# Adapter by roles on one Trainium2 core: the order of the first loads, splits and turns ahead of the steady loop

## The reference

```python
h = einsum('bsh,bhk->bsk', x, W_down[role]) + b_down[role][:, None, :]   # H = 1024 -> K = 512
h = gelu(h, approximate=False)
u = einsum('bsk,bkh->bsh', h, W_up[role]) + b_up[role][:, None, :]       # K = 512 -> H = 1024
y = x + u
yn = (y - mean(y)) * rsqrt(var(y) + 1e-5)                                # over H
out = yn * gamma[role][:, None, :] + beta[role][:, None, :]
```

## Time and profile before

| | us |
|---|---|
| median of three runs | 1424.69 |
| lowest, highest | 1423.2, 1425.12 |
| the profiled execution's own time | 1424.26 |
| its span in the trace | 1422.4 |
| TensorE busy in the span | 1405.7 |
| VectorE busy | 1203.8 |
| ScalarE busy | 782.5 |
| GpSimd busy | 195.1 |

### The profile page before, as it was taken

The page is one execution under the profiler, slowest core; times in us unless marked ns, Lnnn a source line. Parts: engine busy times, 40 slices in busy tenths (PEclk is TensorE's granted clock), DMA queues, the critical chain, the costliest instruction groups (busy, mean ns, idle before and its releaser), DMA issues.

```text
span 1422.4 us, 32330 instructions
## 1 busy us (share of the span) xinstructions
PE 1405.7 (99%) x6175; PEld 1156.3 (81%) x6176; DVE 1203.8 (85%) x1454; ACT 782.5 (55%) x2059; POOL 195.1 (14%) x297
## 2 busy tenths in 40 slices
PE   8999999999999999999999999999999999999997
PEld 6888888888888888888888888888888888888885
DVE  7798988888888888888888899888888888888888
ACT  5555555555555555555555555555555555555555
POOL 3376411100000000000000377310100000000000
PEclk9999999999999999999999999999999999999999
DMA  9688777766666666666666778776776666667663
GB/s 222 177 232 229 217 211 205 199 199 205 185 190 197 196 182 196 196 197 183 188 204 192 209 230 225 222 201 193 204 217 186 197 203 185 184 194 203 187 193 139
DMA packets 208726, 283.52 MB, mean 199 GB/s; under 512 B 25775, under 2 KB 155312, under 8 KB 208702
## 3 DMA queue, kind: packets, MB, share of 16 engines
q1 hardware_dynamic: 201726, 269.60, 63.5%
q0 software_dynamic: 5888, 12.07, 5.1%
q10 hardware_dynamic: 1088, 1.57, 0.4%
HBM read 183.27 MB, written 99.88 MB: 199 GB/s over the span
## 4 chain that ended last, share of the span: by engine, by line
PE 96%; DVE 1%; DMA 1%; issue 1%; ACT 1%; SPq 0%; DVEq 0%
PE p_down L989 16%; PE p_down L990 16%; PE p_down L991 16%; PE p_up L989 16%; PE p_up L990 16%; PE p_up L991 16%; DMA row<-in_L_cond_W_down 0%; DVEq L241 0%; SPq L267 0%; SPq L258 0%; DMA h_quad<-h_dram 0%; DMA h_dram<-h 0%; DVE row L805 0%; PE p_hT L985 0%; DVE x_quad L921 0%
## 5 line engine op out<-in xcount | busy, mean ns | idle before, releaser
L989 PE MATMUL p_down<-wd_hi,xT_hi 128*128 x1012 | 395.4, 391 | 0.2
L991 PE MATMUL p_down<-wd_hi,xT_lo 128*128 x1012 | 393.9, 389 | 0.0
L990 PE MATMUL p_down<-wd_lo,xT_hi 128*128 x1012 | 393.9, 389 | 0.0
L989 PE MATMUL p_up<-wu_hi,hT_hi 128*128 x1008 | 392.7, 390 | 0.1
L991 PE MATMUL p_up<-wu_hi,hT_lo 128*128 x1008 | 392.3, 389 | 0.0
L990 PE MATMUL p_up<-wu_lo,hT_hi 128*128 x1008 | 392.3, 389 | 0.0
L559 ACT ACTIVATE hT_hi<-p_hT 128x512 fp32r<-128x512 f32 x126 | 75.5, 599 | 435.4 <-DVE p_hT L724 432.6
L744 DVE SCALAR_TENSOR_TENSOR row<-p_up,row 128x1024 f32<-128x1024 f32 x126 | 154.2, 1224 | 170.8 <-PE p_up L991 135.1
L989 PEld LDWEIGHTS p_down<-wd_hi,xT_hi 128*128 128x128 f32 x1012 | 189.9, 188 | 45.0 <-issue 5.2
L989 PEld LDWEIGHTS p_up<-wu_hi,hT_hi 128*128 128x128 f32 x1008 | 189.2, 188 | 42.0 <-issue 1.6
L991 PEld LDWEIGHTS p_down<-wd_hi,xT_lo 128*128 128x128 f32 x1012 | 190.0, 188 | 39.9
(11 more groups left out here) (164 smaller groups left out, 955.6 us busy)
## 6 DMA issues: line engine op xcount, KB each, us to landing
x_quad<-in_x SPq DMA_DIRECT2D x510, 128.0 KB, 3.6
row<-in_x SPq DMA_DIRECT2D x126, 512.0 KB, 4.1
out<-row SPq DMA_DIRECT2D x126, 512.0 KB, 2.8
h_dram<-h SPq DMA_DIRECT2D x125, 256.0 KB, 4.3
h_quad<-h_dram SPq DMA_DIRECT2D x500, 64.0 KB, 2.0
w_raw<-in_L_cond_W_down POOLq DMA_DIRECT2D x64, 64.0 KB, 3.7
w_raw<-in_L_cond_W_up POOLq DMA_DIRECT2D x64, 64.0 KB, 3.8
row<-in_L_cond_W_up SPq DMA_DIRECT2D x16, 128.0 KB, 5.8
```

Of the source, the lines that this page charges most:

```text
L989: pe.matmul(dst, a_hi, w_hi, start=first, stop=False)
L990: pe.matmul(dst, a_hi, w_lo, start=False, stop=False)
L991: return pe.matmul(dst, a_lo, w_hi, start=False, stop=last)
```

## The change

ScalarE's queue issues quads 0 and 1 of piece 2 of W_down directly behind piece 1, ahead of the wait for `first_known` and of its two quads of x of sequence 0. Lo of piece 1 is made in two subtractions of 128 x 512 (`split_chunk`), one ahead of `subtract_half(0, 0)` and one behind it, with a semaphore of its own for the first. `transpose_half(0, 1)` moves from behind `transpose_half(0, 0)` to behind `transpose_half(1, 0)`, and `round_half(0, 1)` and `subtract_half(0, 1)` move behind those of (1, 0). GpSimd clears half of `xT_lo`, and TensorE does two matmuls of 512 columns on these zeros ahead of its wait for `first_hi`. Of the four `keep_clock` matmuls behind the spreads two are left, and the second of them waits for `half_hi`, which is the rounding of (0, 0).

```diff
@@ gpsimd
             pool.memset(opener[:, 0:2], 0.0).then_inc(pieces_split, 1)
+            pool.memset(xT_lo[:, 0:HALF, :].bitcast(F32), 0.0).then_inc(zeros_ready, 1)
@@ scalar
             load_first(act, 0, range(1, NQ))
             load_first(act, 1)
+            load_first(act, FD - 2, range(0, NQ // 2))
             act.wait_ge(first_known, 1)
...
             round_first(0)
-            load_first(act, FD - 2, range(0, NQ // 2))
             act.wait_ge(order_in_psum, 1)
...
             round_first(1)
             round_half(0, 0)
-            round_half(0, 1)
             copy_param(2, p_up[1][:, :], BETA, H, beta_loaded)
             copy_param(1, p_hT[:, :], BD, K, bias_loaded)
             round_half(1, 0)
+            round_half(0, 1)
             round_first(2)
@@ vector
+            def split_chunk(n, c, done):
+                buf, hi, lo, _ = first_piece(n)
+                at = slice(c * K, c * K + K)
+                dve.wait_ge(first_hi, n + 1)
+                dve.tensor_tensor(lo[:, at], buf[:, at], hi[:, at].bitcast(F32), ALU.subtract).then_inc(done, 1)
...
             def subtract_half(b, half):
                 hi, lo = half_x(b, half)
+                if (b, half) == (0, 0):
+                    dve.wait_ge(zeros_used, 1)
...
             split_first(0)
             transpose_half(0, 0)
-            transpose_half(0, 1)
+            split_chunk(1, 0, chunk_split)
             subtract_half(0, 0)
-            split_first(1)
+            split_chunk(1, 1, first_split)
             dve.wait_ge(first_known, 2)
             for b in range(2):
                 params_at[b], when_loaded[b] = first_slot(b)
             transpose_half(1, 0)
+            transpose_half(0, 1)
+            subtract_half(1, 0)
             subtract_half(0, 1)
-            subtract_half(1, 0)
             transpose_half(1, 1)
@@ tensor
+            pe.wait_ge(zeros_ready, 1)
+            for _ in range(2):
+                mm = pe.matmul(p_down[:, :], xT_lo[:, 0, :], xT_lo[:, 0:HALF, :], start=True, stop=True)
+            mm.then_inc(zeros_used, 1)
             pe.wait_ge(first_hi, 1)
             keep_clock(2)
...
-            keep_clock(4)
+            keep_clock(1)
+            pe.wait_ge(half_hi, 1)
+            keep_clock(1)
             pe.wait_ge(first_known, 2)
...
                 for c in range(half * HALF, half * HALF + HALF):
-                    if b == 0 and c % (FC // K) == 0:
+                    if (b, c) == (0, FC // K):
+                        pe.wait_ge(chunk_split, 1)
+                    elif (b, c) == (0, FC // K + 1):
+                        pe.wait_ge(first_split, 2)
+                    elif b == 0 and c % (FC // K) == 0:
                         pe.wait_ge(first_split, c // (FC // K) + 1)
```

More of the change, by code:

```diff
@@ L143, in adapter_kernel @@
         param_rows_clear, row_known = sem("param_rows_clear"), sem("row_known")
+        zeros_ready, zeros_used, chunk_split = sem("zeros_ready"), sem("zeros_used"), sem("chunk_split")
         ident_ready, params_spread, params_landed = sem("ident_ready"), sem("params_spread"), sem("params_landed")
```

## The result

The changed kernel takes 1427.68 us (median of 11 runs, 1426.1 to 1430.27) against 1424.95 us (11 runs, 1423.11 to 1425.33): ratio 1.0024, 95% interval 1.0016 to 1.0032. It is slower by 2.7 us, outside the predicted range. The profiled execution took 1426.3 us itself, 2.0 more than the profiled one of before, and is among the quickest of the changed kernel's runs.

What follows compares the result with a forecast made beforehand. The prediction took TensorE (busy 99%) as the bound, with VectorE deciding turn_h(0). Its terms summed to +0.8 us on the profiled 1424.26, 1425.1, set at 1425.2 as the median lies 0.43 above that execution; range 1423.5 to 1426.8.

Steps and rivals of the forecast that it cites:

- TensorE's own program would allow 13.5: Ahead of the first product: keep_clock pair at 8.58, seven spreads and two fillers let TensorE start it at 13.5 us.
- Product (0,0) starts 0.2 behind the subtraction's end ... 13.8: First product on TensorE: starts 0.2 us after VectorE's subtraction ends at 13.6, so at 13.8 us.
- the lower clock: Rival, chance 0.06: a break of some 0.3 us at 13.5 keeps first-product matmuls slow, 2.3 us; sum 3.1, time 1427.4.
- x turned at 11.46: VectorE's turn of sequence 0's x: lands and is turned at 11.46 us instead of 10.40, behind piece 2.
- The dear bound: Delay of sequence 0's x by piece 2: 256 KB at 242 GB/s, 1.06 us; the forecast took this bound.
- the hole is filled: Rival, chance 0.22: piece 2 partly fills the DMA dip at 6 to 7 us, x only 0.57 late; 1424.5 us.
- Even turns: Rival, chance 0.16: DMA queues share evenly, x of sequence 0 lands at 12.5, +1.7 us, time 1426.0.
- The zeros by 3.8: Two TensorE matmuls on zeros: end by 3.8 us, ahead of the sort's first matmul, at no cost.
- Turn of (1,0) at 14.5 with "issue" as releaser: VectorE's turn of (1,0): held by L840's register loads, 1.6 us, until 14.5 instead of 14.06.
- VectorE's chain, 6.4 us to the turn of (2,0): VectorE from turn of (1,0) to turn of (2,0): 6.4 us, ending at 20.9 to 21.0 against 20.17, 0.8 late.
- turn_h(0) at 25.8: TensorE's turn_h(0): starts at 25.8 us instead of 24.99, 0.8 later, set by VectorE's chain.
- every microsecond by which turn_h(0) comes earlier or later stays in the time: From turn_h(0) on: TensorE's matmuls have no hole to hide a shift, so it goes wholly into the time.

Runs made afterwards that it cites:

- e1: Changed kernel with TensorE's three register loads and their wait for first_known moved ahead of the wait for half_hi: 1425.51 us, ratio 1.0007 to the kernel before.
- e6: Kernel before with only piece 2's two quads issued ahead of x on ScalarE's queue: 1423.8 against 1423.61 us, ratio 1.0002.
- e12: e1 with turn, rounding and subtraction of (0,1) in their old place: 1425.21 against 1424.62 us for the kernel before, ratio 1.0007.
- e2: Changed kernel with piece 2's two quads issued behind round_first(0) again, so x goes first: 1424.39 us, ratio 1.0005 to the kernel before.
- e10: Kernel before with only the later turn, rounding and subtraction of (0,1): 1424.66 against 1424.62 us, ratio 1.0000.
- e3: Changed kernel with nine keep_clock matmuls instead of one behind the wait for half_hi: 1425.59 us, ratio 1.0012 to the kernel before.
- e8: e5 with VectorE's register loads for sequences 2 and 3 behind the bias of sequence 0: 1424.36 against 1423.61 us for the kernel before, ratio 1.0002.
- e5: Changed kernel with the edits of e1 and e2 together: 1425.36 against 1423.61 us for the kernel before, ratio 1.001.
- e4: Kernel before with its four keep_clock matmuls replaced by one, the wait for half_hi, and one: 1425.72 us, ratio 1.0007.
- e7: Kernel before with only the zeros added (GpSimd's memset and two matmuls): 1424.1 against 1423.61 us, ratio 1.0001.
- e11: Kernel before with zeros, two fillers instead of four, and VectorE's register loads for sequences 2 and 3 behind sequence 0's bias: 1424.08 against 1424.62 us, ratio 0.9996.

## Why the prediction was wrong

The step that failed is "TensorE's own program would allow 13.5", on which "Product (0,0) starts 0.2 behind the subtraction's end ... 13.8" rests. The subtraction ended at 13.95, and the product started at 15.73. The prediction followed the matmuls of TensorE's program, seven spreads and two fillers, and not the instructions between them. It named what the change queues behind `pe.wait_ge(half_hi, 1)` only as one filler; three register loads stand there too, and with their arithmetic they take 2.3 us. So the break ahead of the product was 2.0 us, where the prediction had "some 0.3 us", and in the profiled execution it brought the lower clock, the rival to which the prediction had given a chance of 0.06. It had applied that very question to VectorE (the loads of L840, priced at 1.6 us) and not to TensorE. e1 moves these loads, and the product, the turns and turn_h(0) come within 0.2 us of the forecast: that step is shown, not argued.

The others, in order:

- *round_first(0) at 7.45*: 7.42, right.
- *x turned at 11.46*: 11.78 in the changed kernel, 11.52 in e1, 11.40 in e6. The dear bound held, so "the hole is filled" fell: the dip was filled (227 GB/s), and x was late all the same. Even turns (12.5) fell too.
- *The zeros by 3.8*: wrong place. They stand behind the sort's last matmul in TensorE's order and ran at 6.74. It cost nothing there.
- *Turn of (1,0) at 14.5 with "issue" as releaser*: 14.94 with "issue" and 14.68 in e1, x being 0.32 and 0.06 later than forecast. Right, the price of 1.6 us too: from the subtraction's start at 13.26, where the loads begin, to the turn it is 1.68 us.
- *VectorE's chain, 6.4 us to the turn of (2,0)*: 6.28 in e1 (14.68 to 20.96), right. It was 6.74 in the changed kernel, since ScalarE's rounding of (1,1) there waited for TensorE (1.61 us).
- *turn_h(0) at 25.8*: 25.76 in e1, 28.32 in the changed kernel.
- *The lower clock*: the right rival in kind and in place, at 0.06 much too small a chance. Its price was 2.3 us and its total 3.1; measured 1.58 us to turn_h(0) (eight steps) and 2.7 in all. Its break was to be "some 0.3 us", which was there (0.33 ahead of the last filler) and did nothing by itself elsewhere: e1 had 0.16 and e12 0.39 ahead of the product, e2 0.43 ahead of the last filler, and all three kept the clock. The 2.0 us behind it are what differs from e1. The prediction's sign that would prove it wrong, matmuls of the first product 0.427 us apart, is what came.
- *Nothing was said of SyncE's queue*, which holds x of sequence 2 behind the turn of (0,1). In the changed kernel it goes out at 16.42 instead of 12.72, W_up at 18.30 instead of 14.59. e10 shows that the like costs nothing, and e12, where x goes out at 13.27, has the same ratio as e1, where it goes out at 16.16. It was luck.
- *"every microsecond by which turn_h(0) comes earlier or later stays in the time"*: not to a microsecond. From turn_h(0) to the last matmul it was 1387.22 us before; against that it took 1.26 less in the changed kernel, 0.97 less in e3, 0.70 less in e1, 0.93 less in e10, 0.84 more in e8 and 2.86 more in e5. The prediction's sum has no term for it. For 0.8 us, the sum of the forecast, such differences are as large as the effect.

Of the result, shown are the place of the loads (e1), the slow steps as a cost of their own (e3, plain in the traces, just short of it in the ratios), and that the late x alone doesn't do it (e6), while the changed kernel with both lies above every run of before in its series (from 1426.1 us on, against 1425.33 at most). That the wait with two fillers fewer can bring slow steps without the rest (e4) is shown in one execution; others are as short as before. That the 2.0 us idle made the clock fall is read from the traces of the changed kernel, e1 and e3; e2's trace, with the same idle time and no fall, shows that it isn't enough. Open are the extra of e5, the time between turn_h(0) and the last matmul, and why executions of e2 and e4 differ so.

## What to carry to other kernels

When a wait is put into an engine's program, list every instruction behind it up to the next one that matters, register loads, assertions and arithmetic with them; they are in no count of busy time, and show only as a gap with "issue" as its releaser, or under a name that is wrong. Load registers ahead of a wait on data, while the array still has matmuls in its queue. And price an idle stretch of TensorE twice, once for itself and once for the steps at the lower clock behind it: here 1.6 us on top, in a trace in which the engine had come to the higher level 1.2 us before the gap (12.5 to 13.7).

## What the runs showed of the hardware

Three register loads with their arithmetic and assertion held TensorE's queue for 2.3 us in each of five kernels (before, changed, e2, e3, e4; 0.49, 0.31 and 0.31 us for the loads themselves, the rest between and behind them). The Trainium skill, page "DMA: Bandwidth & Descriptors", section "Latency and other measured facts", gives about 600 ns as the least time of such a load. By that page three take at least 1.8 us, an estimate. The loads' own records here are shorter than its figure, and the whole sequence, 0.77 us each, is longer.

The same idle stretch of 2.01 us stood ahead of a fall of the clock from 2.4 to 1.2 GHz in the changed kernel's trace and of none in e2's. One difference is what went ahead: in e2 the higher level had come at about 9.7 and matmuls had run from there to 11.2 and again at 11.6; in the changed kernel it had come at about 12.5, followed by two fillers only, one at 12.50 and one at 13.21. Whether that decides it isn't shown. In e4's profiled execution the steps were those of the lower level already ahead of the gap of 1.50 us, and stayed so until 20.1, while the granted clock read 1.00 from 14.2 to 20.1.

When the higher level comes isn't set by TensorE's program alone. In e2, e7, e8 and e11 TensorE starts the zeros at 6.62, the first pair of fillers at 7.66 or 7.67 and the first spread at 8.68 or 8.69, and the steps become short at about 9.7, 10.9, 12.0 and 11.1. That suggests that executions of one program can meet the same gap in different states, and one trace doesn't tell for all of them. In the changed kernel two runs have a mean granted clock of 0.996, and the two slowest, 1429.89 and 1430.27 us, have 0.998, as has e4's longest, in whose trace the steps stay long from the start to 20.1. These two may have taken e4's course; no trace of them shows it. The changed kernel's runs spread over 4.2 us (1426.1 to 1430.27), those of before in the same series over 2.2.
